# Layer 1 of a graph network: the scanned receiver rows go to PSUM through ScalarE and are added by VectorE, instead of entering PSUM by identity matmuls

## The reference

```python
sender_features = nodes[senders]
receiver_features = nodes[receivers]
concat = jnp.concatenate([sender_features, receiver_features, edges], axis=-1)
h = jax.nn.relu(concat @ W1 + b1)
messages = h @ W2 + b2
aggregated = jax.ops.segment_sum(messages, receivers, num_segments=n_nodes)
degree = jax.ops.segment_sum(jnp.ones(...), receivers, num_segments=n_nodes)
aggregated = aggregated / jnp.maximum(degree, 1.0)[:, None]
new_nodes = aggregated + (nodes @ Wn + bn)
```

## Time and profile before

| | us |
|---|---|
| median of 3 runs | 5320.2 |
| the profiled execution | 5303.53 |
| its span (first to last instruction) | 5301.8 |
| layer 1, first gather to last gather | 2774.9 to 5072.4 |
| TensorE busy, of the span | 1752.7 (33%) |
| VectorE busy | 2196.3 (41%) |
| ScalarE busy | 1728.1 (33%) |
| GpSimd busy | 3508.6 (66%) |
| mean granted TensorE clock | 0.608 of full |

### The profile page before, as it was taken

One profiled execution on the slowest core, in us unless ns is written; L12 is line 12 of the kernel. 1 busy time (PEld: TensorE's weight loads), 2 busy tenths in 40 slices (PEclk: granted clock), 3 DMA queues, 4 the chain that ended last, 5 costly groups with the idle time before them and its releaser, 6 DMA issues.

```text
span 5301.8 us, 22035 instructions
## 1 busy us (share of the span) xinstructions
PE 1752.7 (33%) x3727; PEld 739.0 (14%) x3747; DVE 2196.3 (41%) x2960; ACT 1728.1 (33%) x1393; POOL 3508.6 (66%) x3562
## 2 busy tenths in 40 slices
PE   4630000000000000003464455454555555555544
PEld 2210000000000000002231111111111111111113
DVE  3453222222222222225543465454555555455445
ACT  2422111111111111112233454454554555445431
POOL 5567777777777777775547566666666666666634
PEclk7965555555555555555556677676766767677665
DMA  4025333333333333332333344444444444444432
GB/s 165 7 79 170 107 107 107 107 107 107 106 107 107 106 107 106 107 102 85 98 104 116 120 160 140 135 151 133 153 151 140 146 151 152 133 152 150 134 104 79
DMA packets 202250, 635.79 MB, mean 120 GB/s; under 512 B 70347, under 2 KB 72848, under 8 KB 157808
## 3 DMA queue, kind: packets, MB, share of 16 engines
q1 hardware_dynamic: 88624, 457.72, 23.2%
q0 software_dynamic: 113344, 177.81, 14.3%
q10 hardware_dynamic: 256, 0.00, 0.0%
HBM read 335.07 MB, written 300.32 MB: 120 GB/s over the span
## 4 chain that ended last, share of the span: by engine, by line
POOL 29%; another core or an unknown queue 22%; issue 21%; DVE 15%; PE 10%; ACT 1%; DMA 1%; DVEq 1%; ACTq 0%; SPq 0%; POOLq 0%
POOL edge_arena L499 28%; DVE node_arena L1330 11%; PE ps L644 10%; POOL edge_arena L511 1%; ACT node_arena L822 1%; DVE edge_arena L1363 0%; DVE node_arena L1348 0%; DVE ps L1227 0%; POOL edge_arena L597 0%; DVE node_arena L1340 0%; DMA table<-node_arena 0%; DVE node_arena L1228 0%; DMA node_arena<-recv_term 0%; DVE node_arena L1224 0%
## 5 line engine op out<-in xcount | busy, mean ns | idle before, releaser
L597 POOL DMA_INDIRECT edge_arena<-table1s,ix x1568 | 1482.3, 945 | 816.4 <-issue 507.3
L499 POOL DMA_INDIRECT edge_arena<-table,ix x1440 | 1496.8, 1039 | 498.6 <-issue 498.6
L1330 DVE TENSOR_TENSOR_SCAN node_arena<-ps,node_arena 128x510 f32<-128x510 f32 (+1 forms) x980 | 945.5, 1038 | 97.2 <-issue 73.3
L644 PE MATMUL ps<-node_arena,ident 128*128 128x512 f32 x784 | 741.4, 1102 | 356.6 <-issue 247.8
L644 PE MATMUL ps<-w1e_bd,edge_terms 128*128 128x512 f32 x784 | 496.6, 782 | 760.7 <-issue 436.2
L644 PE MATMUL ps<-we_bd,edge_terms 128*128 128x32 f32 x392 | 93.6, 403 | 1885.1 <-issue 1495.1
L1363 DVE TENSOR_TENSOR edge_arena<-edge_arena,ps 128x1024 f32<-128x1024 f32 x196 | 238.6, 1218 | 1001.1 <-remote 806.2
L1170 DVE TENSOR_TENSOR score<-edge_arena,node_wide 128x128 f32<-128x128 f32 x49 | 18.6, 380 | 1466.6 <-DMA edge_arena<-table,ix 1451.0
L951 ACT ACTIVATE node_arena<-edge_arena 128x2048 f32<-128x2048 f32 x98 | 374.6, 3822 | 676.4 <-issue 670.5
L930 ACT ACTIVATE node_arena<-node_arena 128x2048 f32<-128x2048 f32 x98 | 375.3, 3830 | 523.3 <-DMA node_arena<-recv_term 450.7
L834 ACT ACTIVATE ps<-expo 128x128 f32<-128x128 f32 x49 | 13.8, 281 | 1402.8 <-issue 1244.6
(11 more groups left out here) (199 smaller groups left out, 1845.9 us busy)
## 6 DMA issues: line engine op xcount, KB each, us to landing
recv_term<-zeros SPq DMA_DIRECT2D x98, 1024.0 KB
node_arena<-recv_term SPq DMA_DIRECT2D x98, 1024.0 KB
rows<-edge_arena SPq DMA_DIRECT2D x98, 1024.0 KB
rows<-edge_arena SPq DMA_DIRECT2D x49, 1152.0 KB
edge_arena<-table,ix POOLq DMA_INDIRECT x1568
edge_terms<-e32g_d SPq DMA_DIRECT2D x98, 256.0 KB
edge_arena<-table1s,ix POOLq DMA_INDIRECT x1568
edge_terms<-e16g_d SPq DMA_DIRECT2D x49, 256.0 KB
```

The source lines that it names most:

```text
L499: pool.indirect_dma_start(G0[slot][:, u, :], None, table0, bass.IndirectOffsetOnAxis(ap=ix[slot][:, u:u + 1], axis=0)).then_inc(gathered0[ ...
L597: pool.indirect_dma_start(G1[slot][:, u, :], None, table1s, bass.IndirectOffsetOnAxis(ap=ix[slot][:, u:u + 1], axis=0)).then_inc(gathered1 ...
L644: return pe.matmul(out_, lhsT, rhs, start=start, stop=stop)
L1330: last = scan(F[:, lo:hi], hold[:, 0:hi - lo], F[:, lo:hi], 0.0, ALU.mult, ALU.add)
```

## The change

TensorE does only the edge terms, one bank for four edges, in banks 6 and 7 in turn (`EDGES_AT`, `EDGES` = 2). ScalarE copies the scanned receiver rows of a chunk, turned back to time by feature, into PSUM banks 2 to 5, in two halves of 1024 (`turn_1`). VectorE makes six adds a chunk (`adds1`): for each half two edge banks of 512 and then the two banks of receiver rows, 1024. The semaphore `edge1_mm` now counts single banks, four a chunk; `turned1` counts ScalarE's halves; `edge_added` and `recv_added` count VectorE's adds. In SyncE's chunk the store of the rows now stands ahead of the load of edge features, which waits for `edge1_mm`. The loops of PE, ACT and DVE over the chunks are written out in Python; those of SP and POOL are not touched.

```diff
-            def edge1(c, s, it):
-                r = s % 2
-                pe.wait_ge(e32_in[s], it * 16 + 16)
+            def edge1(c):
+                pe.wait_ge(e32_in[c % RING1], 16 * (c // RING1) + 16)
                 for g in range(4):
-                    if g % 2 == 0:
-                        pe.wait_ge(half_used[g // 2], c + 1)
-                    mm(ps[:, 2 + g, :], edge_terms[s][:, g, :], w1e_bd[:, :], True, False)
-                pe.wait_ge(scanned_x, c + 1)
-                for g in range(4):
-                    recv = F1_f[XF1[r]][:, :, 1 + 4 * g:5 + 4 * g].rearrange("p f t -> p t f")
-                    last = mm(ps[:, 2 + g, :].rearrange("p (t f) -> p t f", f=HID), ident[:, :], recv, False, True)
-                    if g % 2:
-                        last.then_inc(edge1_mm, 1)
+                    n = 4 * c + g
+                    if n >= EDGES:
+                        pe.wait_ge(edge_added, n - EDGES + 1)
+                    mm(ps[:, EDGES_AT + n % EDGES, :], edge_terms[c % RING1][:, g, :], w1e_bd[:, :]).then_inc(edge1_mm, 1)
...
+            def turn_1(c):
+                act.wait_ge(scanned_x, c + 1)
+                for h in range(2):
+                    if c:
+                        act.wait_ge(recv_added, 2 * c + h - 1)
+                    act.activation(ps[:, TURNS_AT + 2 * h:TURNS_AT + 2 * h + 2, :].rearrange("p a (t f) -> p (a t) f", f=HID),
+                                   F1_f[XF1[c % 2]][:, :, 1 + HT * h:1 + HT * h + HT].rearrange("p f t -> p t f"),
+                                   ACT.Copy).then_inc(turned1, 1)
+
+            def turn1(c):
+                turn_1(c)
+                if c + 1 < K1:
+                    if c:
+                        act.wait_ge(turned1, 2 * c)
                     act.wait_ge(led_x, c + 1)
-                    act.wait_ge(edge1_mm, c * 2 + 2)
-                    recv_1(c + 1, 1 - r)
...
+            def adds1(c):
+                dve.wait_ge(gathered1[c % RING1], (c // RING1 + 1) * (16 * C1))
+                rows = lambda lo, n: G1[c % RING1][:, lo:lo + n, :].rearrange("p t f -> p (t f)")
+                for h in range(2):
+                    for g in (2 * h, 2 * h + 1):
+                        pre = rows(QT * g, QT)
+                        dve.wait_ge(edge1_mm, 4 * c + g + 1)
+                        tt(pre, pre, ps[:, EDGES_AT + g % EDGES, :], ALU.add).then_inc(edge_added, 1)
+                    pre = rows(HT * h, HT)
+                    dve.wait_ge(turned1, 2 * c + h + 1)
+                    dve.wait_ge(edge_added, 4 * c + 2 * h + 2)
+                    tt(pre, pre, ps[:, TURNS_AT + 2 * h:TURNS_AT + 2 * h + 2, :].rearrange("p a b -> p (a b)"),
+                       ALU.add).then_inc(recv_added, 1)
...
-                if loads:
-                    sp.wait_ge(edge1_mm, c * 2 + 4)
-                    sp.dma_start(edge_terms[s][:, :, :], e32g[:, bass.ds(c * 4 + 4 * RING1, 4), :]).then_inc(e32_in[s], 16)
                 if stores:
                     store1(c - 1, 1 - s % 2)
+                if loads:
+                    sp.wait_ge(edge1_mm, c * 4 + 4)
+                    sp.dma_start(edge_terms[s][:, :, :], e32g[:, bass.ds(c * 4 + 4 * RING1, 4), :]).then_inc(e32_in[s], 16)
```

More of the change, by code:

```diff
@@ L240, in build @@
         FEATS = BANK // T1
-        hold1 = [ps[:, r, 0:FEATS * T1] for r in range(2)]
+        HOLDS = 2
+        TURNS_AT, EDGES_AT, EDGES = HOLDS, HOLDS + 4, 2
+        QT, HT = C1 // 4, C1 // 2
+        hold1 = [ps[:, r, 0:FEATS * T1] for r in range(HOLDS)]
         hold1_f = [h.rearrange("p (f t) -> p f t", t=T1) for h in hold1]
@@ L937, in turn1 @@
[L937 to L949 removed]
+                act.wait_ge(rows1_stored[c % 2], 16 * (c // 2) + 16)
@@ L950, in turn1 @@
+            def turn1(c):
[3 more added lines that the diff above has]
+                        act.wait_ge(turned1, 2 * c)
+                    act.wait_ge(led_x, c + 1)
+                    recv_1(c + 1)
+                if c:
+                    rows_1(c - 1)
+                if HOLDS <= c + 1 < K1:
+                    hold_1(c + 1)
+                act.wait_ge(recv_added, 2 * c + 2)
+                if c:
                     act.wait_ge(rows1_ready, c)
-                act.activation(F1_f[HF1[r]][:, :, 1:T1].rearrange("p f t -> p t f"), G1[s], ACT.Relu).then_inc(relu_done, 1)
@@ L958, in _ @@
-            recv_1(0, 0)
-            turn1(0, 0, c_later=False)
-            with act.Fori(0, K1 // RING1 - 1) as it:
-                for i in range(RING1):
-                    turn1(it * RING1 + (i + 1), (i + 1) % RING1)
-            for c in range(K1 // RING1 * RING1 - RING1 + 1, K1):
-                turn1(c, c % RING1, c + RING1 < K1, c + 1 < K1)
-            rows_1(K1 - 1, (K1 - 1) % 2)
+            for c in range(HOLDS):
+                hold_1(c)
+            recv_1(0)
+            for c in range(K1):
+                turn1(c)
@@ L968, in turned @@
+            rows_1(K1 - 1)
             def turned(k, r):
@@ L1000, in _ @@
             dve.sem_inc(pds_out, 2)
-            for h in range(2):
-                dve.sem_inc(half_used[h], 1)
             dve.sem_inc(agg_used, 1)
@@ L1352, in turn1 @@
                 dve.wait_ge(hold1_ready, c + 1)
-                if first:
-                    dve.memset(F1_f[HF1[1]][:, :, C1:T1], 0.0)
-                scan1(F1[XF1[r]], hold1[r], scanned_x)
-                if not first:
-                    sums1(c - 1, 1 - r)
-                with_b2(c)
-                dve.wait_ge(gathered1[s], it * (16 * C1) + 16 * C1)
-                for h in range(2):
-                    pre = G1[s][:, 8 * h:8 * h + 8, :].rearrange("p t f -> p (t f)")
-                    dve.wait_ge(edge1_mm, c * 2 + (h + 3))
-                    tt(pre, pre, ps[:, 2 + 2 * h:4 + 2 * h, :].rearrange("p a b -> p (a b)"), ALU.add).then_inc(half_used[h], 1)
@@ L1365, in _, with sums1 @@
-            turn1(0, 0, 0, first=True)
-            with dve.Fori(0, K1 // RING1) as it:
-                for i in range(RING1):
-                    turn1(it * RING1 + (i + 1), (i + 1) % RING1, it + (i + 1) // RING1)
-            turn1(K1 - 1, (K1 - 1) % RING1, (K1 - 1) // RING1)
+                scan1(F1[XF1[c % 2]], hold1[c % HOLDS], scanned_x)
+            def sums1(c):
+                dve.wait_ge(scanned1, c + 1)
+                dve.tensor_copy(F1_f[HF1[c % 2]][:, :, 0:1], F1_f[HF1[1 - c % 2]][:, :, C1:T1]).then_inc(led_h, 1)
+                dve.wait_ge(led_h, c + 1)
+                dve.wait_ge(relu_done, c + 1)
+                scan1(F1[HF1[c % 2]], hold1[c % HOLDS], scanned1)
@@ L1370, in _ @@
+            dve.memset(F1_f[HF1[1]][:, :, C1:T1], 0.0)
+            for c in range(K1):
+                receivers1(c)
+                if c:
+                    sums1(c - 1)
+                with_b2(c)
+                adds1(c)
             for col in range(K1, NB):
                 with_b2(col)
-            lead1(K1 - 1, (K1 - 1) % 2)
-            sums1(K1 - 1, (K1 - 1) % 2)
+            sums1(K1 - 1)
             dve.wait_ge(rg0_in[0], 16 * NB // 2)
```

59 lines of the change are left out of this document (17 added, 42 removed).

## The result

The changed kernel takes 5232.0 us (median of 4 runs, 5223.26 to 5239.45), the kernel before 5319.4 us beside it: ratio 0.9837, 95% interval [0.9809, 0.9865]. It is faster, by 87 us or 1.6%, where I forecast 307, and it lies above my range. The profiled execution's span fell from 5301.8 to 5237.7 us.

The account below looks back on a forecast made before the run. GpSimd's gathers (20.0 us a chunk) were the floor, with pauses from TensorE's late passes. From 5303.5 us: pauses -338, +39, end -15, edges +7 give 4996; plus 16.7 is 5013, rounded to 5010; range 4955 to 5190.

Parts of the forecast that it names:

- The floor: GpSimd's layer 1 gathers: 1.25 us apart, 20.0 us a chunk, 1960 us in all, leaving 338 us of pauses.
- The pauses: GpSimd's waits for the index copy nearly vanish; gathers span about 2000 us and become VectorE's largest layer 1 wait.
- TensorE's passes: Layer 1: passes retire at 2.6 us each while gathers run; 16 to 8 cuts 42 to 21 us a chunk.
- 0.4 us a chunk: Layer 1 gathers: 20.4 us a chunk taken, between bounds 20.0 and TensorE's 21.0; +39 us over 98 chunks.
- The first rival: Layer 1: part of the stalls stays, 22.0 us a chunk, total about 5175 us; chance 0.19.
- ScalarE and VectorE: Added layer 1 work: 1.9 us per ScalarE half, 0.73 per 512-wide add; each engine about 15.8 us a chunk, under 20.
- lap of the chain: From scan to next scan through ScalarE's turns and copies: 16.8 us, 3.2 to spare below 20.0.
- SyncE and X1: Layer 1 loads: one more issue adds about 3 us, within the spare; as slower rival 24.1 us, about 5375, chance 0.11.
- The end of layer 1: After the last gather: the consumer lags less, up to 27 us won, 15 taken.
- The loops written out: Chunk loops: register instructions go and code grows; both costed at nothing, hidden under 20 us a chunk.
- The chances: Whole kernel: faster by over 0.3% 0.83, within 0.05, slower 0.12; forecast case itself 0.64.

Follow-up runs that it names:

- e7b: Changed kernel without layer 1's receiver and edge terms, so GpSimd's gathers never wait for buffers, on a slower chip: 5167.6 us.
- e15: Changed kernel with two X1 buffers, recv_1 and hold_1 moved ahead, and four edge adds made two of 1024: 5207.9 us, ratio 0.9771.
- e1: Kernel before without the identity matmuls (receiver terms missing), edge matmuls in their place behind the scan, 8 TensorE passes a chunk: 5154.4 us, ratio 0.9685.
- e6b: Changed kernel with a two-column TensorE matmul ahead of each edge matmul, on a slower chip: 5358.5 us, ratio 1.0057.
- e5b: Changed kernel with two buffers for X1, each load issued two chunks ahead, on a slower chip: 5239.6 us, ratio 0.9827.
- e12: Kernel before with two buffers for X1, each load issued two chunks ahead: 5322.1 us, ratio 0.9992.
- e7: Changed kernel without layer 1's receiver and edge terms, so gathers never wait for buffers, on the quick chip: 4569.9 us.

## Why the prediction was wrong

- **The floor: this is the step that failed.** I wrote "16 of them need 20.0 us, and 98 chunks 1960 us. So 338 us of layer 1 are pauses of GpSimd" and counted all 338 as removable. The distance of 1.25 us is that of gathers fresh from a pause. Alone they need 2168 us (e7b), so 130 of the 338 were to be had. The pauses of the kernel before hid this: between them every row I had taken showed 1.25, and where a kernel has fewer pauses its gathers are slower (e15, e1, e7b). Against the profiled execution (5239.5, I had summed 4996) the miss is 243: 208 from this term (2168 less 1960), 25 from the end, 7 from the late start of the gathers (13.9 for 7, less than starts differ between profiles), 4 from what stays above the floor.
- **The pauses: the forecast's sign of being right failed.** I expected them nearly to vanish and VectorE's largest wait to be for the gathers. In the changed kernel they are still some 218 of the 250 us above 1960, and VectorE's waits for gathers are 16.6 us in all, while those for updates that the profile calls remote are 192.9 (L1357) and 125.8 (L1325). That the miss comes out as the floor's 208 and only 4 besides is bookkeeping against what could be reached, not what the trace shows GpSimd doing.
- **TensorE's passes: held in kind.** Taking 8 of 16 passes away removed TensorE from the path (the adds that wait for it have 98.5 us idle, was 1001), and doubling their number by tiny ones brought the loss back. The size of 2.6 us a pass is near the 2.4 of e6b's stall; in e1's chunk it is 2.0 (8 passes from 3703.86 to 3719.84). But what is late after the change are VectorE's updates, not TensorE's. I had put what is left above the floor at 0.4 us a chunk; it was 0.44 (22.56 less 22.12), 0.29 and 0.28 in the other two profiles. That is luck: I had worked it out from TensorE's 21.0 us a chunk.
- **The first rival** (part of the stalls stays, 22.0 us a chunk, 5175) came nearest, in its number and in what the trace shows: 39 pauses stayed. It did not have the floor, by which taking the rest of them away can give at most 44 us (2210.6 less 2168). Its own sum gives 5170 and not 5175.
- **ScalarE and VectorE: right.** 1.975 us a half (1.9 taken), 0.683 us an add of 512 (0.73 taken), lap of the chain 16.84 with half the gathers (16.8 taken).
- **SyncE and X1: right that it doesn't decide.** Two buffers for X1 change nothing (e5b, e12).
- **The end of layer 1: wrong sign.** I took -15; behind the last gather lie 9.9 us more than before. In e1, where VectorE does wait for the gathers, it is 204.3 us (229.4 before), 25 less and near the 27 that I had worked out for such a consumer. The changed kernel's consumer still lags behind GpSimd.
- **The loops written out, costed at nothing.** They were not tried alone; e1, which keeps the hardware loops, gained more than the changed kernel.
- **The chances.** Faster was right. Nothing in the range allowed for a floor other than 20.0, though layer 0 stood beside it in the page; with 22.1 in the place of 20.0 the same sum gives 5218 (5010 and 208), though that is said afterwards.

Open is what links the two: gathers that slow to 1.40 us when GpSimd never pauses, and updates of TensorE, or else of VectorE, that come late. e1 has both at once. Both are absent on the quick chip. A path that all of them share and that is full on the slower chips would explain it, and that a pause of GpSimd or fewer gathers clear it speaks for that, but no run measured such a path. The transfers themselves are hardly slower: the packets of the gathers' queue took 18.6% of the 16 DMA engines' time over 2168 us in e7b and 20.1% over 1959 us in e7, which is 0.129 and 0.126 us a packet (an estimate from these shares and some 50160 packets). Untested is also whether the recording of instructions takes part: every run here is listed with a span and a granted clock, as such records give them, so none here shows the kernel without them. Open is also what the 27 to 44 us above the floor are made of.

## What to carry to other kernels

Take the pace of a repeated instruction from a stretch in which its engine never pauses, however far away in the program, and not from the distance of two neighbours; where the engine pauses often, the pauses may be paying for the pace. Before a bottleneck's removal is priced, price the next floor with the same care. And a time on one chip is of that chip: the same kernel took 4577 and 5320 us, and on the quick chip this change should be worth nothing, though it was not run there, since two versions of it stand at 0.9998 and 1.0021 of the kernel before.

## What the runs showed of the hardware

- Indirect DMAs of GpSimd (128 rows of 512 bytes) went out 1.25 us apart for 174 of them and then 1.40 us in the mean when nothing made GpSimd pause (e7b; e1 the same in all, 2168.8 us); in layer 0 they took 1.386 us in the mean on each of the slower chips. On the quick chip it was 1.25 us throughout.
- On the slower chips, while gathers ran without long pauses, a semaphore update came 1.4 to 4.3 us late on VectorE (slow lap of the changed kernel), and TensorE's up to 15.6 us behind the end of its records (kernel before, 4036.4 to 4052.01 in the earlier trace rows), late passes or late updates. With half the gathers and a pause of 7.1 us in each chunk hardly any was late.
- A TensorE pass of two columns, 0.24 us of matmul and its weight load, cost there about as much as one of 512: 784 such records took the changed kernel, at 0.978 to 0.984 of the kernel before, to 1.0057; on the quick chip such a kernel stood at 1.0021.
